# The tokenizer's window scores: a pair of heads per 32-row group with ScalarE's two masked key copies, in place of GpSimd's twelve masked blocks

## The reference, cut to what matters

```python
qkv = (y @ qkv_w + qkv_b).reshape(B, nW, WIN, 3, NH, dh)     # B=16, nW=1, WIN=64, NH=12, dh=16
q, k, v = (qkv[:, :, :, 0], qkv[:, :, :, 1], qkv[:, :, :, 2])
scores = jnp.einsum('bwqhd,bwkhd->bwhqk', q, k) * dh ** (-0.5)
a = jax.nn.softmax(scores, axis=-1)
o = jnp.einsum('bwhqk,bwkhd->bwqhd', a, v).reshape(B, N, D)
return o @ proj_w + proj_b
```

## Time and profile before

| | us |
|---|---|
| median of 3 runs | 627.84 |
| the three runs | 624.95, 627.84, 631.99 |
| span of the profiled execution | 626.2 |
| TensorE busy | 569.1 (91%) |
| VectorE busy | 435.2 (69%) |
| ScalarE busy | 293.3 (47%) |
| GpSimd busy | 70.4 (11%) |
| mean granted clock of TensorE | 0.956 of full speed |

### The profile page before, as it was taken

How to read it: one execution, slowest core, us unless ns; L and a number is a source line. 1 busy time by engine, 2 the same in 40 slices (tenths; PEclk the granted TensorE clock), 3 DMA queues, 4 the chain that set the end, 5 groups by cost and what they waited for, 6 DMA issues and landing times.

```text
span 626.2 us, 10251 instructions
## 1 busy us (share of the span) xinstructions
PE 569.1 (91%) x4137; PEld 399.6 (64%) x4137; DVE 435.2 (69%) x879; ACT 293.3 (47%) x392; POOL 70.4 (11%) x72
## 2 busy tenths in 40 slices
PE   4998989878989999999999999999958999989786
PEld 4766567566677665776876655776836557683465
DVE  4224776698558748977768838977728888847982
ACT  0243444535245546647445446647434546623653
POOL 6032200001110200110010300110000020010000
PEclk9998999969988999999998999999987999999989
DMA  9992010000000000100000000000000000000000
GB/s 216 291 198 80 1 58 1 7 2 1 1 0 2 1 1 4 49 7 2 1 20 0 3 1 1 0 2 1 2 20 1 0 1 2 1 21 0 1 2 19
DMA packets 12669, 15.95 MB, mean 25 GB/s; under 512 B 6427, under 2 KB 10046, under 8 KB 12238
## 3 DMA queue, kind: packets, MB, share of 16 engines
q1 hardware_dynamic: 9710, 12.71, 8.1%
q10 hardware_dynamic: 2400, 2.00, 1.0%
q0 software_dynamic: 512, 0.59, 0.5%
HBM read 14.11 MB, written 1.18 MB: 24 GB/s over the span
## 4 chain that ended last, share of the span: by engine, by line
PE 64%; DVE 16%; issue 7%; SPq 5%; ACT 4%; DMA 3%; POOL 1%; DVEq 0%; ACTq 0%; POOLq 0%
PE ps L627 17%; PE ps L631 11%; PE ps L902 8%; PE ps L960 4%; DVE smax L1578 3%; SPq L528 3%; PE ps L725 3%; DMA w_cproj<-in_cproj 3%; PE ps L1068 2%; PE ps L1087 2%; DVE pr L1580 2%; PE ps L784 2%; PE ps L1044 2%; PE ps L617 2%; DVE psum L1589 1%
## 5 line engine op out<-in xcount | busy, mean ns | idle before, releaser
L1578 DVE TENSOR_REDUCE smax<-ps 96x12 f32<-96x1152 f32 x32 | 43.1, 1348 | 29.1 <-PE ps L950 18.4
L1253 ACT ACTIVATE pr<-pr 96x1152 f32<-96x1152 f32 x28 | 32.6, 1163 | 46.7 <-DVE pr L1580 46.7
L627 PE MATMUL ps<-w_cqkv,side_c 128*128 128x512 f32 (+1 forms) x102 | 44.7, 570 | 1.1 <-DVE pr L1580 1.1
L960 PE MATMUL ps<-w_ident,pr 96*96 96x96 f32 x336 | 35.4, 259 | 6.7 <-DVE pr L1601 5.0
L1259 ACT ACTIVATE pT<-ps 96x1152 f32<-96x1152 f32 x28 | 31.5, 1126 | 20.1 <-PE ps L960 20.1
L960 PEld LDWEIGHTS ps<-w_ident,pr 96*96 96x96 f32 x336 | 30.4, 133 | 13.8 <-issue 8.8
L1589 DVE TENSOR_REDUCE psum<-pr 96x12 f32<-96x1152 f32 x28 | 37.6, 1341 | 2.0 <-ACT pr L1253 2.0
L1580 DVE TENSOR_TENSOR pr<-ps,smax 96x1152 f32<-96x1152 f32 x28 | 37.9, 1353 | 1.0
L1286 ACT ACTIVATE squares<-ps 128x1536 f32<-128x1536 f32 x12 | 17.4, 1452 | 37.4 <-PE ps L631 37.4
L1680 DVE TENSOR_REDUCE ss<-squares 128x24 f32<-128x1536 f32 x12 | 21.0, 1746 | 13.1 <-ACT squares L1286 13.1
L631 PE MATMUL ps<-w_cqkv,side_c 64*128 64x512 f32 (+1 forms) x102 | 28.5, 575 | 0.0
(11 more groups left out here) (366 smaller groups left out, 1313.8 us busy)
## 6 DMA issues: line engine op xcount, KB each, us to landing
x_in<-in_xT SPq DMA_DIRECT2D x3, 768.0 KB, 4.5
b_kB<-in_cqkv SPq DMA_DIRECT2D x1, 1152.0 KB
w_cqkv<-in_cqkv SPq DMA_DIRECT2D x2, 567.0 KB
w_cqkv<-in_cqkv SPq DMA_DIRECT2D x1, 864.0 KB
out<-side_c ACTq DMA_DIRECT2D x3, 288.0 KB, 2.3
heads<-in_xT ACTq DMA_DIRECT2D x3, 256.0 KB, 3.8
side_in<-in_patchT SPq DMA_DIRECT2D x3, 192.0 KB, 4.3
side_tff<-in_tok_ff SPq DMA_DIRECT2D x1, 576.0 KB, 8.2
```

Of the source, the lines that this page charges most:

```text
L627: pe.matmul(out_ap, lhs(n, 0, slice(0, 128)), rhs(n, 0, slice(0, 128)), start=banks[n] not in banks[:n], stop=False)
L960: m = pe.transpose(t[0:N, h // 4, (h % 4) * N:(h % 4 + 1) * N], w.y.pr[:, s % 2, h * N:(h + 1) * N], w_ident[0:N, 0:N])
L1253: act.activation(w.y.pr[:, s % 2, :], w.y.pr[:, s % 2, :], ACT.Exp, scale=head ** -0.5)\
L1578: dve.tensor_reduce(mx, t, AX.X, ALU.max).then_inc(w.S[stage + "_sub"], 1)
```

## The change

The scores of the tokenizer are made the way the next attention makes them. ScalarE writes two key copies straight from PSUM, each with a per-partition scale (`w_parity`) and bias (`tok_k_bias`), four ACTIVATEs in place of the two of `a_kT`, and then the two of `a_qT`; GpSimd's step `a_s` goes. TensorE makes, per half of the group, 12 products (6 pairs x 2 images) of 32 rows, 64 weight columns and 128 moving columns in place of 4. The scores take three banks in place of two, and pair 3 waits through `a_mid` for pair 2. The heads then lie in the order of `PAIR_AT`, which `a_o` follows. VectorE reads three banks of 256 columns in place of two banks. The parity and the tokenizer's key bias are made in `a_bc`, early, in place of `a_wc.0`, and for that the two mask loads go ahead of `w_pe` in SP's queue. The table of steps stays as it is.

```diff
@@ BANKS and READ_BY @@
-    "a_s": 2,
+    "a_s": 3,
-    "a_qk": lambda k: [("a_qkT", 4)],
+    "a_qk": lambda k: [("a_qkT", 2), ("a_kB", 4)],
@@ SP @@
             sp.dma_start(w_ident[:, :], ident).then_inc(loads["ident"], 16)
+            sp.wait_ge(s_pad, 2)
+            for dst, src in ((w_mask[0:HC, 0:6], mask), (w_mask[HC:128, 6:8], mask[0:128 - HC, 0:2])):
+                sp.dma_start(dst, src).then_inc(loads["mask"], 16)
             split_rows(sp, "vec", w_pe, peT)
-            sp.wait_ge(s_pad, 2)
-            for dst, src in ((v128[:], vec128), (w_mask[0:HC, 0:6], mask), (w_mask[HC:128, 6:8], mask[0:128 - HC, 0:2]),
-                             (w_prio[:], prio), (w_ff2_b[:], ffn2_b), (w_cproj_b[:], cproj_b)):
+            for dst, src in ((v128[:], vec128), (w_prio[:], prio), (w_ff2_b[:], ffn2_b), (w_cproj_b[:], cproj_b)):
@@ TensorE, a_s @@
                 pe.wait_ge(w.S["a_qkT"], w.upto("a_qkT", w.a))
-                pe.wait_ge(w.S["a_kB"], w.upto("a_kB", w.a, 2 * t2 + 2))
-                for c, (rows, heads_of) in enumerate(A_PARTS):
+                pe.wait_ge(w.S["a_kB"], w.upto("a_kB", w.a))
+                for pair in (0, 1, 2, 4, 5, 3):
+                    c, r = pair // 4, slice(pair % 4 * 32, pair % 4 * 32 + 32)
+                    bank, second = PAIR_AT[pair]
+                    if pair == 3:
+                        pe.wait_ge(w.S["a_mid"], w.upto("a_mid", w.a, t2 + 1))
                     for half in range(2):
-                        s = 2 * t2 + half
-                        m = pe.matmul(t[64 * half:64 * half + NI, heads_of.start * NI:heads_of.stop * NI],
-                                      w.x.a_qT[0:rows, c, s * NI:(s + 1) * NI],
-                                      w.x.a_kB[0:rows, heads_of, half * NI:(half + 1) * NI], start=True, stop=True)
+                        at = slice((2 * t2 + half) * NI, (2 * t2 + half + 1) * NI)
+                        m = pe.matmul(t[64 * half:64 * half + NI, bank, second * 2 * NI:(second + 1) * 2 * NI],
+                                      w.x.a_qT[r, c, at], w.x.a_kB[r, :, c, at], start=True, stop=True)
+                    if pair == 2:
+                        m.then_inc(w.S["a_mid"], 1)
@@ ScalarE, a_qk @@
-                act.activation(w.x.a_kT[:, 0, :], t[:, 0, TA:2 * TA], ACT.Identity, bias=bias_col("tok_k"))\
-                   .then_inc(w.S["a_qkT"], 1)
-                act.activation(w.x.a_kT[0:64, 1, :], t[64:128, 1, 0:TA], ACT.Identity, bias=bias_col("tok_k", 1, 64))\
-                   .then_inc(w.S["a_qkT"], 1)
+                if w.first:
+                    act.wait_ge(s_tok_k, 3)
+                for odd in range(2):
+                    act.activation(w.x.a_kB[:, odd, 0, :], t[:, 0, TA:2 * TA], ACT.Identity,
+                                   scale=w_parity[:, odd:odd + 1], bias=tok_k_bias[:, odd, 0:1]).then_inc(w.S["a_kB"], 1)
+                    act.activation(w.x.a_kB[0:64, odd, 1, :], t[64:128, 1, 0:TA], ACT.Identity,
+                                   scale=w_parity[0:64, odd:odd + 1], bias=tok_k_bias[0:64, odd, 1:2])\
+                       .then_inc(w.S["a_kB"], 1)
@@ VectorE, out of a_wc.0 and into a_bc @@
-                    dve.tensor_reduce(w_parity[:, :], w_mask[:, :].rearrange("p (j two) -> p two j", two=2), AX.X, ALU.add)\
-                       .then_inc(s_set, 1)
-                    dve.wait_ge(s_set, 5)
...
+                dve.wait_ge(loads["mask"], 16 * n_loads["mask"])
+                dve.tensor_reduce(w_parity[:, :], w_mask[:, :].rearrange("p (j two) -> p two j", two=2), AX.X, ALU.add)\
+                   .then_inc(s_tok_k, 1)
+                dve.wait_ge(s_tok_k, 2)
+                for c, rows in ((0, 128), (1, 64)):
+                    m = dve.tensor_tensor(tok_k_bias[0:rows, :, c], w_parity[0:rows, :],
+                                          bias_col("tok_k", c, rows).to_broadcast([rows, 2]), ALU.mult)
+                m.then_inc(s_tok_k, 1)
@@ GpSimd @@
-            def a_s(w, t2):
-
-                if w.first:
-                    pool.wait_ge(loads["tables"], 16 * n_loads["tables"])
-                if t2 == 1:
-                    pool.wait_ge(fill_sem(w, ("a_s", 0)), fill_count(w, ("a_s", 0)))
-                else:
-                    pool.wait_ge(w.S["a_qkT"], w.upto("a_qkT", w.a, 2))
-                for c, (rows, heads_of) in enumerate(A_PARTS):
-                    shape = [rows, heads_of.stop - heads_of.start, 128]
-                    pool.tensor_tensor(w.x.a_kB[0:rows, heads_of, :],
-                                       w.x.a_kT[0:rows, c, t2 * 128:(t2 + 1) * 128].unsqueeze(1).to_broadcast(shape),
-                                       w_mask[0:rows, 0:shape[1]].unsqueeze(2).to_broadcast(shape), ALU.mult)\
-                        .then_inc(w.S["a_kB"], 1)
```

More of the change, by code:

```diff
@@ L121 @@
 PSUM_BANKS = 8
-BANKS = {"a_em": 1, "a_x0": 1, "a_f1": 3, "a_f2": 1, "a_h2": 1, "a_qk": 2, "a_v": 1, "a_s": 2, "a_pt": 2,
+BANKS = {"a_em": 1, "a_x0": 1, "a_f1": 3, "a_f2": 1, "a_h2": 1, "a_qk": 2, "a_v": 1, "a_s": 3, "a_pt": 2,
          "a_o": 1, "a_ot": 1, "a_pr": 1, "a_ht": 3, "a_u": 2, "a_in": 3, "a_out": 1, "b_u": 2, "c_u": 2, "b_qk": 3, "b_v": 2, "a_pb": 1, "a_tb": 1, "a_bc": 1, "heat": 1,
@@ L130 @@
     "a_h2": lambda k: [("hT", 3) if k else ("x1T", 3)],
-    "a_f2": lambda k: [("hT", 1) if k else ("x1T", 1)], "a_qk": lambda k: [("a_qkT", 4)],
+    "a_f2": lambda k: [("hT", 1) if k else ("x1T", 1)], "a_qk": lambda k: [("a_qkT", 2), ("a_kB", 4)],
     "a_v": lambda k: [("a_vB", 1)], "a_s": lambda k: [("a_sub", 2 * k + 2)], "a_pt": lambda k: [("a_pT", k + 1)],
@@ L222 @@
 SHARED = {**{n_: "early_" + early for n_, early in zip(PER_C, [n_ for n_ in PER_A if n_ not in TO_SP])},
-          **{"late_" + n_: before for n_, before in zip(PER_C, [n_ for n_ in PER_A if n_ not in LATEST])}}
+          **{"late_" + n_: before for n_, before in zip(PER_C, [n_ for n_ in PER_A if n_ not in LATEST])},
+          "a_mid": "early_a_mid"}
 def base(name):
@@ L278, in program @@
         k_bias = sb("k_bias", [128, 2, 2])
+        tok_k_bias = sb("tok_k_bias", [128, 2, 2])
         ones_row = sb("ones_row", [128, 2])
@@ L310, in program @@
         a_h = a_wide.rearrange("p (c t) -> p c t", t=TA)
-        a_kB = a_wide.rearrange("p (h t) -> p h t", h=NH)
+        a_kB = a_wide[:, 0:2 * 2 * TA].rearrange("p (o c t) -> p o c t", o=2, c=2)
         attn = sb("attn", [128, 3 * 2 * TA + 2 * NH * NI + NH // 2 * 128])
-        x1T, a_qT, a_kT = (attn[:, n * 2 * TA:(n + 1) * 2 * TA].rearrange("p (c t) -> p c t", c=2) for n in range(3))
+        x1T, a_qT = (attn[:, n * 2 * TA:(n + 1) * 2 * TA].rearrange("p (c t) -> p c t", c=2) for n in range(2))
         a_p = attn[:, 6 * TA:6 * TA + 2 * NH * NI].rearrange("p (two n) -> p two n", two=2)
@@ L418, in program @@
         S.update({name: S[first] for name, first in SHARED.items()})
-        loads = {n: sem("load_" + n) for n in ("patch0", "patch1", "patch2", "vec", "tables", "tff1", "tff2", "tqkv", "tproj", "in", "out", "qkv",
+        loads = {n: sem("load_" + n) for n in ("patch0", "patch1", "patch2", "vec", "tables", "mask", "tff1", "tff2", "tqkv", "tproj", "in", "out", "qkv",
                                                "proj", "ff1", "ff2", "cqkv", "cproj", "ident", "cols")}
-        n_loads = {"patch0": 2, "patch1": 2, "patch2": 2, "vec": 9, "tables": 6, "tff1": 4, "tff2": 1, "tqkv": 16, "tproj": 4, "in": 4, "out": 1, "qkv": 16,
+        n_loads = {"patch0": 2, "patch1": 2, "patch2": 2, "vec": 9, "tables": 4, "mask": 2, "tff1": 4, "tff2": 1, "tqkv": 16, "tproj": 4, "in": 4, "out": 1, "qkv": 16,
                    "proj": 2, "ff1": 4, "ff2": 1, "cqkv": 7, "cproj": 6, "ident": 1, "cols": 12}
@@ L429, in program @@
         s_pad = sem("zeros")
+        s_tok_k = sem("tokenizer_key_bias")
         s_heat = sem("zeros_for_heat")
@@ L809, in a_o @@
                         m = pe.matmul(t[64 * half:64 * half + NI, n * k:(n + 1) * k],
-                                      w.x.a_pT[:, n, half * NI:(half + 1) * NI], w.x.a_vB[:, 2 * t2 + half, n, :],
+                                      w.x.a_pT[:, 2 * PAIR_AT[n][0] + PAIR_AT[n][1], half * NI:(half + 1) * NI],
+                                      w.x.a_vB[:, 2 * t2 + half, n, :],
                                       start=True, stop=True)
@@ L1835, in c_u @@
                 pool.tensor_tensor(w.y.out_rows[:, :, :], hx[:, :, :], bias, ALU.add).then_inc(w.S["h2b"], 1)
-            run(pool, {"a_en": a_en, "a_ht": a_ht, "a_out": a_out, "b_f2": b_f2, "a_s": a_s, "b_pr": b_pr, "c_u": c_u})
+            run(pool, {"a_en": a_en, "a_ht": a_ht, "a_out": a_out, "b_f2": b_f2, "b_pr": b_pr, "c_u": c_u})
 def positions():
```

28 lines of the change are left out of this document (14 added, 14 removed).

## The result

| | before | changed |
|---|---|---|
| median of the runs beside each other, us | 627.94 (20 runs) | 634.12 (20 runs) |
| fastest and slowest, us | 623.01, 632.66 | 629.95, 637.27 |
| ratio, with its 95% interval | | 1.0093, 1.0068 to 1.0117 |
| span of the profiled execution, us | 626.2 | 630.1 |
| mean granted clock | 0.956 | 0.946 |

By the ratio the changed kernel is 0.93% or 5.8 us slower (6.2 by the medians), where 0.3 us was forecast. Every ratio in this document leaves out executions more than 1.5% above the fastest of the same kernel, among them two of the old kernel's with 816 and 938 us, at granted clocks of 0.64 and 0.55.

What follows compares the result with a forecast made beforehand. TensorE, busy for 91% of the span, was taken to bound the kernel. Group 1's -1.5 plus 0.9 in each of groups 2 and 3 gave +0.3 us: 626.5 on the span, 628.1 as median, range 623.5 to 632.5.

Steps and rivals of the forecast that it cites:

- the sum: Whole kernel: -1.5 in group 1 plus 0.9 in each of groups 2 and 3, +0.3 us on the profiled span.
- group 1's -1.5: Group 1: both score steps 0.70 us shorter, VectorE's weight step some 0.1 sooner, ScalarE has room; together -1.5 us.
- The score step: TensorE's tokenizer scores: a new step takes 0.90 us, 0.70 shorter than the old (bounds 0.2 and 1.15).
- The two halves run side by side: TensorE's scores: the images' halves overlap, 0.90 us per step; the rival, one behind the other, 1.38 and 630.1 us, chance 0.11.
- ScalarE: `a_qk`: six ACTIVATEs take 3.19 us, 1.36 more, so TensorE waits 1.2 longer ahead of `b_pr.0` in groups 2 and 3.
- The third bank: Groups 2 and 3: `a_o.0` on bank 7 must wait for VectorE's subtraction of `a_s.1`, 0.9 us later per group.
- without the bank wait: Groups 2 and 3 end about 0.1 us earlier each; as the rival "only the bank wait is missing", 626.1 us, chance 0.09.
- What TensorE saves in group 0 it waits away there: Group 0, before 53 us: the `w_cproj` load and VectorE's weight step set the end, so its two score steps gain nothing.
- The start: Mask loads ahead of `w_pe`: up to 1 us delay for VectorE is absorbed by later waits; zero, up to 0.2 either way.
- The clock: Rival: new TensorE idle in groups 2 and 3 lowers the clock, 1.7 us per fall, one per group, 631.5 us; chance 0.19.
- GpSimd: Group 1: without GpSimd beside it, VectorE's second weight step shrinks from 3.27 to near 2.6 us, off the path, counted nothing.

Runs made afterwards that it cites:

- the repeat: The changed kernel run once more, unaltered, beside the old kernel on the same chip, with a second profile: ratio 1.0074 (1.0034 to 1.0114).

## Why the prediction was wrong

The step that failed is the one on the clock: the sum priced the new waits of groups 2 and 3 at +0.9 each and gave nothing for a fall of the granted clock behind them. The runs have one fall of 10 us in group 2, which costs 3.75 us. The second term that failed is group 1's -1.5, which was +0.4 in the profiled pair. Term by term:

**The score step.** Right: 0.93 to 1.00 us at full clock against 0.90. The two halves run side by side, that rival is out.

**ScalarE.** Right: from 212.57 to the last end at 215.76 are 3.19, as forecast, and the wait ahead of `b_pr.0` is 1.53 against "some 1.6". Two key copies of 0.56 start 0.59 apart. The rule of the Trainium skill (ScalarE: Activation LUTs, What ACT_TABLE_LOAD costs) that ACTIVATEs behind each other overlap by about 93 ns doesn't hold for them; the two q copies, 0.37 apart at 0.47 each, do follow it. In the old kernel the copies before them, with bias alone and 0.47 long, started 0.50 apart, so the scale isn't what decides. (By that rule the prediction's own working gives a group some +0.5, not the +0.6 that it names; nothing hangs on it.)

**The third bank.** Right: `a_o.0` waits, 0.64 us at full clock where 0.9 was forecast; alone, on the old kernel, 0.92. The sum for groups 2 and 3, +0.9 each, measured +0.8 at full clock; without the bank wait -0.1 was forecast and +0.1 measured. Nothing in the queueing argument of these two groups failed.

**Group 1.** Wrong: "the first at half clock, where the work saved is worth 0.70 again if the half-clock stretch (57.80 to 64.60) ends where it does". It doesn't. The stretch is 10.2 or 13.7 us long in the kernels with the new scores, and 6.8, 6.8 and 10.2 in the profiles with the old ones; the 1.5 forecast is 1.3 at full clock, and nothing with the stretch. The step "What TensorE saves in group 0 it waits away there" left out that the waits around `w_cproj` have a price of their own, which filling them gave back (4.6 us of the piece). Whether the work saved in group 0 makes the stretch longer wasn't tested.

**The start.** "Zero, with up to 0.2": VectorE's first step is 0.9 late, and at the end of the `w_cproj` wait the profiled pair is 0.4 apart. Over all profiles that point lies at 53.6 to 55.5 with the old start (four profiles) and 54.0 to 56.2 with the new (eight), 0.7 more in the mean; the changed kernel with the mask loads behind `w_pe` has 55.3, inside both. Whether any of the 0.7 is the change's stays open. The early stretch at 0.50 isn't the change's own: two of those four old profiles have one.

**The clock.** I had the mechanism as a rival at 0.19, with one fall of 1.7 us per group, and set against it that "the old stretch had its small idle times there and stayed at full speed". The old idle ahead of `b_pr.0` was 0.44 us, the new 1.53. One fall costs 3.75, not 1.7. What I mis-sized is the length: I took 3.4 us from the earlier trace rows, and the clock stayed at 0.50 for 10.2 although TensorE was busy throughout. (The price by length was too high: I took half, measured is 3.75 of 10.2, 37%.) And I asked whether it falls, where the runs ask how often: in group 2 it fell in three of four profiles of kernels with both waits (changed, mask loads behind `w_pe`, changed with group 1 filled; not in the repeat), in group 3 in none of the four. What decides between a fall and none isn't known. 3/4 x 3.75 + 2 x 0.8 + 0.4 (group 1) is 4.8, beside 5.8 and, in the repeat, 4.7 measured by the ratios. (By the means of all executions the repeat is only 2.8 us slower, 631.2 against 628.4.)

The executions without a profile say the same in another way. Their mean granted clock is 0.946 for the 20 of the changed kernel and 0.953 for 86 of the old one's in the later runs. As an estimate that is 9.5 us more at 0.50 in the changed kernel (twice the missing share, times the span). At 37%, as in group 2, these cost 3.5 us; at the 45% of a line through the old kernel's 86 times and clocks, 4.2. That leaves 1.6 to 2.3 of the 5.8 us for the waits, which the pieces have at 2 x 0.8.

**GpSimd.** VectorE's second weight step without GpSimd beside it:

```profile
67.57 2.56 DVE L1736 TENSOR_TENSOR w_cqkv<-w_cqkv,b_kB 128x2304 f32<-128x2304 f32 x1
```

2.56 against 3.27, as forecast, and off the path.

## What to carry to other kernels

When an edit lets TensorE wait 1 us more ahead of dense work, ask first what clock the next dense stretch will have, and price a fall by the length of the whole stretch at 0.50 (here 37% of 10.2 us), not by the wait. A dummy product in a wait that no dependence can shorten tells in one run whether the wait or its aftermath costs, and may stay in the kernel. Compare such kernels at full clock piece by piece, and take two profiles before a stretch at 0.50 is called the kernel's own.

## What was not expected of the hardware

The same wait (1.53 us, in the same place of the same program) was followed by 10 us at 0.50 in one execution and by none in another. Being busy for 9.68 of 10.00 us did not bring the clock back within that stretch; in the repeat TensorE was busy for 8.49 of 10.00 and stayed at full clock. And three dummy products, 2.4 us of useless work, shortened a piece of 18.4 us by 4.6.
